# Attention of an audio tower: order of the engines, PSUM banks and buffers of a head pair written out

## The reference

```python
def _L0_attn_ref(x, W_Q, b_Q, W_K, b_K, W_V, b_V, W_O, b_O):      # x = layernorm(h), 192 wide, 12 heads of 64
    q = jnp.einsum('bqd,hdm->bqhm', x, W_Q) + b_Q
    k = jnp.einsum('bkd,hdm->bkhm', x, W_K) + b_K
    v = jnp.einsum('bkd,hdm->bkhm', x, W_V) + b_V
    scores = jnp.einsum('bqhm,bkhm->bhqk', q, k) / jnp.sqrt(64)
    scores = jnp.where(causal, scores, -100000.0)
    z = jnp.einsum('bhqk,bkhm->bqhm', jax.nn.softmax(scores, axis=-1), v)
    return jnp.einsum('bqhm,hmd->bqd', z, W_O) + b_O
```

## Time and profile before

| | |
|---|---|
| median of three runs | 1685.71 us |
| profiled execution: its own time, its span | 1688.44 us, 1686.7 us |
| mean granted TensorE clock | 0.931 of full speed |
| TensorE matmul busy | 1461.1 us, 87% |
| VectorE, ScalarE, GpSimd busy | 1091.1, 772.9, 413.7 us |
| attention, first stacked score to the last copy of batch 0 | 205.4 to 371.9 us |

### The profile page before, as it was taken

How to read it: one execution, slowest core, us unless ns; L and a number is a source line. 1 busy time by engine, 2 the same in 40 slices (tenths; PEclk the granted TensorE clock), 3 DMA queues, 4 the chain that set the end, 5 groups by cost and what they waited for, 6 DMA issues and landing times.

```text
span 1686.7 us, 31187 instructions
## 1 busy us (share of the span) xinstructions
PE 1461.1 (87%) x10191; PEld 977.8 (58%) x10192; DVE 1091.1 (65%) x2482; ACT 772.9 (46%) x1490; POOL 413.7 (25%) x431
## 2 busy tenths in 40 slices
PE   5987799999987799999986899989876999959997
PEld 3443477786433577784443677784433777745665
DVE  6988545457987455567897455559885555583553
ACT  2654455543654455524563555516643555432332
POOL 3000233313000234312000343302002456722222
PEclk7999799997989799997998999989989999968999
DMA  5996122210000122201000222200001453212221
GB/s 126 351 351 200 34 46 59 50 34 34 8 0 1 38 64 46 64 11 40 1 1 0 66 46 64 46 2 29 0 1 27 108 129 88 62 37 67 63 63 32
DMA packets 112867, 104.96 MB, mean 62 GB/s; under 512 B 55133, under 2 KB 103322, under 8 KB 112786
## 3 DMA queue, kind: packets, MB, share of 16 engines
q1 hardware_dynamic: 83570, 55.32, 13.7%
q10 hardware_dynamic: 25744, 39.62, 7.1%
q0 software_dynamic: 3472, 8.97, 1.6%
HBM read 29.57 MB, written 47.40 MB: 46 GB/s over the span
## 4 chain that ended last, share of the span: by engine, by line
PE 46%; DVE 32%; issue 12%; ACT 5%; POOL 3%; SPq 2%; DMA 1%; POOLq 0%; DVEq 0%; ACTq 0%
PE ps L1912 12%; DVE arena L1323 10%; PE ps L1963 6%; DVE arena L1321 6%; PE ps L1886 5%; PE ps L1898 5%; PE ps L1854 5%; DVE bn L1481 4%; PE ps L2010 2%; DVE arena L1350 2%; PE ps L1861 2%; ACT arena L1029 1%; SPq L588 1%; POOL out L920 1%; DMA arena<-arena 1%
## 5 line engine op out<-in xcount | busy, mean ns | idle before, releaser
L1963 PE MATMUL ps<-arena,cwt 128*128 128x504 f16 (+2 forms) x1776 | 389.2, 378 | 40.3 <-DVE arena L1321 36.6
L1963 PEld LDWEIGHTS ps<-arena,cwt 128*128 128x128 f16 x1776 | 172.2, 101 | 257.3 <-DVE arena L1321 39.9
L1342 DVE TENSOR_REDUCE nmax<-ps 128x1 f32<-128x128 f32 (+5 forms) x288 | 176.8, 614 | 176.7 <-PE ps L1889 176.6
L1912 PE MATMUL ps<-arena 128*128 128x64 f32 (+2 forms) x2016 | 259.1, 269 | 8.2 <-DVE arena L1350 4.8
L1912 PEld LDWEIGHTS ps<-arena 128*128 128x128 f32 (+2 forms) x2016 | 240.6, 188 | 25.0 <-issue 13.9
L1323 DVE TENSOR_TENSOR arena<-arena 128x1008 f16<-128x1008 f32 (+4 forms) x200 | 227.0, 1135 | 6.9
L1350 DVE COPY arena<-ps 128x512 f32<-128x512 f32 (+4 forms) x288 | 155.6, 540 | 84.3 <-PE ps L1898 79.2
L988 ACT ACTIVATE arena<-ps,nmax 128x128 f32<-128x128 f32 (+5 forms) x288 | 180.3, 626 | 39.4 <-DVE nmax L1342 38.7
L1886 PE MATMUL ps<-arena 128*128 128x512 f16 (+6 forms) x780 | 163.8, 313 | 29.7 <-ACT arena L1029 16.4
L1061 ACT ACTIVATE arena<-ps 128x1008 f32<-128x1008 f32 (+1 forms) x112 | 96.0, 866 | 178.5 <-PE ps L1963 178.5
L1898 PE MATMUL ps<-ident,arena 128*128 128x128 f32 (+2 forms) x1008 | 165.0, 281 | 11.0 <-ACT arena L1029 6.0
(11 more groups left out here) (290 smaller groups left out, 2263.9 us busy)
## 6 DMA issues: line engine op xcount, KB each, us to landing
slot_scratch<-empty_slot ACTq DMA_DIRECT2D x1, 38692.5 KB, 120.6
arena<-arena SPq DMA_DIRECT2D x96, 187.5 KB, 3.0
arena<-arena SPq DMA_DIRECT2D x96, 93.8 KB, 2.3
arena<-in_L_ffn_w SPq DMA_DIRECT2D x16, 288.0 KB, 5.5
arena<-in_L_ffn_w SPq DMA_DIRECT2D x8, 576.0 KB, 5.9
arena<-slot_scratch SPq DMA_DIRECT2D x31, 96.5 KB, 1.9
arena<-slot_scratch SPq DMA_DIRECT2D x31, 96.0 KB, 1.9
xa<-in_x POOLq DMA_DIRECT2D x4, 468.8 KB, 4.8
```

The source lines that it names most:

```text
L1342: v.reduce_max(nmax[0:m, k_:k_ + 1], slot(g)[0:m, 0:128 * i + m], AX.X, negate=True).then_inc(S["smax_done"], 1)
L1912: last = t.matmul(slot(g)[0:m, Z_AT:Z_AT + DH], probt[k % 2][0:kk, c, 0:m], vt[0:kk, c, DH * hh:DH * hh + DH], start=c == 0, stop=c == i)
L1963: last = t.matmul(bank(g, k)[:, 0:c * PITCH].rearrange("p (r c) -> p r c", c=PITCH), cwt[layer][:, w, tap, :], parts[x][:, f:f + 2 * c - 1 ...
```

## The change

The five looped pairs and the sixth become one list per engine, written out for all six pairs (no loop in attention on any engine; wait values are constants). The lists come from three order strings; a name with k of 12 or more belongs to the next pair. EX and MX of a pair are no longer tied to the PSUM ring's order. The PSUM ring becomes two rings of four single banks: banks 0 to 3 for S, Q, K, V, ZT (one bank for tiles 0 to 3, two adjacent ones else), banks 4 to 7 for PT; z goes into the first bank of its own P^T. `prob` has four buffers and `probt` three; the two new ones are `xnt0` and `xnt1`, which only the post phase used. DMA stacking of head 0 now waits until head 0's last score has been made. The last batch drops weight loads and splits that nobody reads.

```diff
-def pair_jobs(last):
-    jobs = []
-    for k in range(STEPS):
-        ahead = k + 2
-        if ahead < STEPS:
-            jobs.append(("s", (ahead,), (ACT_ENGINE,)))
-        elif ahead == STEPS + 1 and not last:
-            jobs.append(("s", (STEPS,), (ACT_ENGINE,)))
-        if k in (TT - 1, TT) and not last:
-            jobs.append(("q" if k == TT - 1 else "k", (), (ACT_ENGINE,)))
-        jobs.append(("pt", (k,), (DVE_ENGINE, ACT_ENGINE) if TILE_ORDER[k % TT] >= 4 else (DVE_ENGINE,)))
-        if k:
-            jobs.append(("z", (k - 1,), (ACT_ENGINE,)))
-    ...
+PE_ORDER = ("PT0 S2 PT1 S3 Z0 S4 PT2 S5 Z1 Z2 S6 S7 PT3 Q PT4 K Z3 Z4 S8 PT5 S9 PT6 PT7 Z5 S10 S11 PT8 Z6 Z7 Z8 "
+            "PT9 PT10 PT11 S12 S13 Z9 Z10 Z11 V ZT").split()
+ACT_ORDER_OF_PAIR = ("CA1 EX2 ZC0 EX3 EX4 ZC1 EX5 EX6 ZC2 CA3 EX7 QC KC ZC3 ZC4 EX8 CA7 ZC5 EX9 ZC6 EX10 ZC7 EX11 ZC8 CA9 "
+                     "EX12 ZC9 EX13 ZC10 ZC11 VC").split()
+DVE_ORDER = ("CP0 MX2 CP1 RC0 MX3 RC1 CP2 MX4 MX5 RC2 MX6 MX7 RC3 CP3 RC4 CP4 MX8 RC5 CP5 CP6 RC6 MX9 RC7 CP7 MX10 "
+             "MX11 RC8 CP8 RC9 CP9 RC10 MX12 RC11 CP10 CP11 MX13 TC").split()
+PROBS, PROBTS = 4, 3
+S_BANKS, P_BANKS = 4, 4
...
+def attention_banks():
+    banks, at_s, at_p = {}, 0, 0
+    for kind, p, k in ATT_PE:
+        if kind == "PT":
+            n = 2 if tile_of(k) >= 4 else 1
+            banks[kind, p, k] = [S_BANKS + (at_p + j) % P_BANKS for j in range(n)]
+            at_p += n
+        elif kind == "Z":
+            banks[kind, p, k] = banks["PT", p, k][:1]
+        else:
+            n = 1 if kind == "S" and tile_of(k) < 4 else 2
+            if at_s + n > S_BANKS:
+                at_s = 0
+            banks[kind, p, k] = list(range(at_s, at_s + n))
+            at_s = (at_s + n) % S_BANKS
+    return banks
...
-        prob = [take(TT * 128) for _ in range(PROBS)]
-        probt = [take(TT * 128).rearrange("p (t c) -> p t c", c=128) for _ in range(2)]
+        prob = [take(TT * 128) for _ in range(3)] + [xnt0]
+        probt = [a.rearrange("p (t c) -> p t c", c=128) for a in (take(TT * 128), take(TT * 128), xnt1)]
...
+            def banks_free(job, b):
+                takers = TAKERS[job]
+                by_act = [ACT_NTH[x] for x in takers if x[0] not in ("CP", "TC")]
+                by_dve = [DVE_NTH[x] for x in takers if x[0] in ("CP", "TC")]
+                if by_act:
+                    wait(pe, "act_freed", ATT, max(by_act), b)
+                if by_dve:
+                    wait(pe, "dve_freed", ATT, max(by_dve), b)
...
-                with pe.Fori(0, PAIRS - 1) as pr:
-                    for n, (kind, args, who) in enumerate(JOBS[PAIR]):
-                        attention_job(PAIR, n, kind, args, b, pr)
-                for n, (kind, args, who) in enumerate(JOBS[LAST_PAIR]):
-                    attention_job(LAST_PAIR, n, kind, args, b)
+                for kind, p, k in ATT_PE:
+                    attention_step(kind, p, k, b)
```

More of the change, by code:

```diff
@@ L248, in split_unit_of, with at @@
     return (layer, next(c for c in range(len(NORM_CHUNKS[layer])) if row < sum(NORM_CHUNKS[layer][:c + 1])))
[L251 to L255, removed]
+def at(sem, phase, k, b=None):
+    setup, tower, att, post, last_post = COUNTS[sem]
     if phase == SETUP:
         return k
-    period = before_last + last_pair + post
+    period = tower + att + post
     if phase == MOE:
         return setup + BATCH * period - post + last_post + k
[L261 to L288, removed]
+    return b * period + setup + {TOWER: 0, ATT: tower}.get(phase, tower + att) + k
 def freed(phase, engine, n):
-    if engine == ACT_ENGINE and phase in (PAIR, LAST_PAIR):
-        return ACT_ORDER[phase].index(n) + 1
     return sum(engine in job[2] for job in JOBS[phase][:n + 1])
@@ L1698, in _, with slot_free @@
             t = nc.tensor
[L1700 to L1713 removed]
+            def slot_free(phase, n, b=None):
                 if phase == SETUP and n < 4:
@@ new lines, in banks_free, with attention_step @@
+            def banks_free(job, b):
[6 more added lines that the diff above has]
+                    wait(pe, "dve_freed", ATT, max(by_dve), b)
+            def attention_step(kind, p, k, b):
+                job = kind, p, k
+                i, hh = tile_of(k), k // TT
+                m = tile_rows(i)
+                banks_free(job, b)
+                if kind in "QKV":
+                    wait(pe, "w_split", ATT, p - 1, b)
+                    last = project(kind.lower(), [bank_at(x) for x in BANKS[job]])
+                elif kind == "S":
+                    places = banks_at(job)
+                    if p == 0 and k < FIRST_SCORES:
@@ L1917, in attention_job @@
-                    wait(pe, "act_freed", phase, freed(phase, ACT_ENGINE, done), b, pr)
-                    for i in range(TT):
-                        m = tile_rows(i)
-                        last = t.transpose(slot(g)[:, 128 * i:128 * i + m], z[0:m, i, :], ident[0:m, 0:m])
+                    assert kind == "ZT"
+                    wait(pe, "act_freed", ATT, ACT_NTH["ZC", p, STEPS - 1], b)
+                    for n in range(TT):
+                        m = tile_rows(n)
+                        last = t.transpose(banks_at(job)[:, 128 * n:128 * n + m], z[0:m, n, :], ident[0:m, 0:m])
```

522 lines of the change are left out of this document (243 added, 279 removed).

## The result

The changed kernel takes 1639.72 us (median of 4 runs, 1636.38 to 1647.61) against 1685.2 (4 runs): ratio 0.9734, interval 0.9692 to 0.9776, 45 us faster. The forecast was 1615, its range 1601 to 1648: the measured time lies inside it, but 25 us above the forecast, with 45 of the 70 us won.

A forecast was written before the change was run, and what follows sets the result against it. TensorE was taken to set the pace, with 3.7 us of stalls in each 28.42 us pair. Savings of 50 (inner pairs), 15 (first) and 5 (last) sum to 70 off 1685.7 us: 1615, range 1601 to 1648.

The forecast's parts named there:

- Stalls, not busy time, as the bound: TensorE in a looped pair: 24.7 us of work in 28.42, so 3.7 us are stalls, half hidden in tails.
- "Busy is busy" (C): TensorE's tails are real work and only the shown 2.0 us idle can go: 1655 us, chance 0.07.
- The walk of the order: TensorE's new order: waits of 0.30 (S2), 0.07 (S3), 0.12 (PT9), 0.11 (S12) remain; period 25.3 us, 3.12 less.
- Last pair: Sixth pair of each batch: 19.0 us of work plus waits make 20.7 against 21.95, saving four times 1.25, 5 us.
- Waits of the next Q: TensorE's next Q behind GpSimd's weight split: no stall, 0 us, bounds 0 and 0.5 in four last-batch pairs.
- Rival B: Stacking before the next pair's first score needs 12.63 us, not 11.24: 1.4 us more in 20 pairs, 1643, chance 0.10.
- Clock: nothing to win: TensorE's granted clock is already 1.00 in looped pairs, so the term adds nothing to the sum.
- First pairs: First pair of each batch, stack landing to first TC: 26.1 us instead of 29.9, saving 3.8, four times 15.
- Dropped loads and splits: 0 on the path: Last batch: leaving out unread weight loads and splits saves 0 us on the path.
- Written-out loops: TensorE's 46 register operations per looped pair, 1.5 us, go; counted as 0, bounds 0 and 1.5 us a pair.
- the sum of 70: Total forecast gain: 50 us from sixteen inner pairs, 15 from first pairs and 5 from last pairs.
- inner pairs of the first three batches: Twelve pairs within the sixteen inner pairs, predicted to save 37.4 us.

The follow-up runs named there:

- experiments 1 and 2: Last batch, each against the changed kernel: expert loads issued right behind the head stacks, 1616.9 us; 22 unread matmuls filling TensorE's stands in two pairs, 1634.96 us.
- experiment 3: The changed kernel with its ring of score banks starting at bank 1 instead of bank 0: 1633.21 us.
- experiment 8: The kernel before, with the last batch leaving out the weight split and load that nobody reads: 1678.65 us, ratio 0.9946.
- experiment 5: The changed kernel with three buffers of P and two of P^T, as before, and the score ring starting at bank 1: 1672.89 us.
- experiment 6: The changed kernel with two banks for every score, so that the score ring holds two scores at a time: 1681.69 us.

## Why the prediction was right, and where its terms were not

**Stalls, not busy time, as the bound: right.** The spacing fell by 3.6 us in most inner pairs, though TensorE had shown only 2.0 us idle. "Busy is busy" (C), which had a spacing above 26.5, is refuted. The work itself was sized too high. The 24.7 us and the waits below, 0.64 us together, do not both fit into 24.83. By the distances between starts in one pair of the changed kernel (259.38 to 284.19) the work is 24.2: scores and masks take 5.2 us for the predicted 5.5, and the passes of Z 8.9 for 9.1. That is the 0.5 us by which the pairs came out shorter than the forecast.

**The walk of the order: right to a tenth.** TensorE around a pair's start and end in the changed kernel:

```profile
258.96 0.27 PE L1871 MATMUL ps<-ident,arena 128*128 128x128 f32 x1
259.38 0.39 PE L1861 MATMUL ps<-arena 128*128 128x256 f16 x2
...
274.50 1.90 PE L1881 MATMUL ps<-arena 128*128 128x64 f32 x16
276.36 1.55 PE L1871 MATMUL ps<-ident,arena 110*128 110x110 f32 x13
277.96 0.27 PE L1861 MATMUL ps<-arena 128*128 128x128 f16 x2
```

S2 should start 0.11 us after PT0 and starts 0.42 after: 0.31 (predicted 0.30). The 16 passes from 274.50 end at 276.23 and PT9 starts at 276.36: 0.13 (0.12). The 13 transposes from 276.36 end at 277.76 by the pace and S12 starts at 277.96: 0.2 at most (0.11). S3 shows nothing (0.07). Pairs of 25.05 to 25.42 us that were looked at (three) have a wait of 0.3 to 0.6 us for the stack's DMA at S12, the spot where the walk had no slack. The mean of the twelve is 25.0, predicted 25.3. Last pair 20.7, predicted 20.7: there Z3 waits 0.65 us (predicted 0.8) and ZT 0.50 (0.6).

**The step that failed** is in *Waits of the next Q*: "In the last batch GpSimd has 4.3 us more per pair behind this split", bounds 0 and 0.5 us in each of four pairs. The work of GpSimd was looked at, and the expert transfers that SyncE issues between the weight load and the stack were not. They were in the rows of SyncE before. The new order brings the k stack to 2.9 us behind them, and the stand then costs twice in two of three pairs, once as itself and once as clock: 22.0 us over three pairs (34.02, 27.96 and 34.47 less three times 24.83) (experiments 1 and 2). Rival B was right in kind, at S12 for the stack, but it was priced for every pair at 1.4 us; it came in three of twenty, at up to 9.6. "Clock: nothing to win" was true and beside the point, as there was something to lose.

**First pairs: term mis-sized.** 8.1 us for 15, because the walk took the steady pattern of banks for the first pair as well; experiment 3 returns 1.5 us in the first pair of batch 0 and 6.5 in all four, of 1.6 to 1.9 missing in each. That its 26.2 us then meets the 26.1 is in part luck: the same stretch of a later pair is 24.6 us (259.38 to 283.97) and not 25.1, and the first pair takes 1.6 us more than that and not 1.0.

**Tail: not seen.** "Dropped loads and splits: 0 on the path" missed 9.7 us. VectorE's additions are 7.65 of them, and experiment 8 shows their cause: the split that was put at 0 kept GpSimd at work on w2 beside them. The other 2 us were not traced.

**Written-out loops: 0 was too low.** In the old order they give 0.57 us a pair. What they give in the new one was not tried.

**Taken together** the sum of 70 came out as 52 in the profiled execution by two terms that were forecast too low (inner pairs of the first three batches, tail), two too high (last batch, first pairs) and 3.6 us of the rest that has no cause here. The range held since it reached over rival B, which had been priced for another cost in other pairs, and since 13 us of unforeseen gain stood against 27.5 us of forecast gain that did not come: in part luck.

## What to carry to other kernels
Read the pace from distances between starts and multiply by counts: the difference to the span is an estimate of what an order can win (here 3.7 us a pair by the count, of which 3.6 came), whatever the busy share says; then walk the new order by hand, bank by bank, for the first turn too, which has another pattern. When a step is moved earlier, list every DMA that its queue carries just ahead of its new place, in every batch that differs, because a transfer that lands late on TensorE's path can cost its own length again in clock. Order, banks and buffers belong together: here any two without the third gave 1% or less, or made it slower.

## What the runs showed of the hardware that was not expected
- VectorE's fp32 additions of 128 x 192, all in SBUF, took 0.35 us each with GpSimd idle, and 2.12 us (median of six) and up to 2.5 beside GpSimd's tensor-tensor instructions of 128 x 1152. These last 2.11 and 2.37 us each, so an addition took about as long as one of them, and they took no longer for it.
- A stack DMA issued 2.9 us behind four expert transfers (1.73 MB) of the same queue landed after 7.50 us, others of the kind after 3.20.
- After stands of 4.4 and 5.2 us TensorE ran at a granted clock of 0.5 for some 9 to 10 us (1309.5 to 1319.8: 0.51); after one of 3.2 us (the pair of 27.96 us) it stayed at 1.00. The length of a stand alone does not decide it: in experiment 5 the clock fell behind stands of 2.03, 2.65 and 2.98 us, in experiment 6 behind one of 2.77. What else does was not looked into.
